# Block 1's edge pass of a graph network on one Trainium2 core: two products in bf16 with three-part factors instead of fp32

## The reference, cut to what matters

```python
def _L1_gnn_ref(x, edge_index, W, b):
    row, col = (edge_index[0], edge_index[1])
    msg = jax.nn.relu(jnp.concatenate([x[row], x[col]], axis=-1) @ W.T + b)
    agg = jax.ops.segment_sum(msg, row, num_segments=x.shape[0])
    out = jax.nn.relu(jnp.concatenate([x, agg], axis=-1) @ W.T + b)
```

## Time and profile before

| | us |
|---|---|
| median of 3 runs | 16247.92 (16245.1 to 17099.07) |
| the profiled execution, its time | 16245.7 |
| its span | 16244.0 |
| DVE busy / ACT busy / POOL busy / PE busy | 6528.5 / 5590.2 / 10961.6 / 8570.5 |
| phase e1, from TensorE's first transpose to ScalarE's last copy | 5065.01 to 5971.29 |

### The profile page before, as it was taken

The page is one execution under the profiler, slowest core; times in us unless marked ns, Lnnn a source line. Parts: engine busy times, 40 slices in busy tenths (PEclk is TensorE's granted clock), DMA queues, the critical chain, the costliest instruction groups (busy, mean ns, idle before and its releaser), DMA issues. The chain is left out here.

```text
span 16244.0 us, 250527 instructions
## 1 busy us (share of the span) xinstructions
PE 8570.5 (53%) x72124; PEld 7859.4 (48%) x72124; DVE 6528.5 (40%) x23629; ACT 5590.2 (34%) x12958; POOL 10961.6 (67%) x11452
## 2 busy tenths in 40 slices
PE   6555541655656974444432433442444444788886
PEld 4555541555556973333332333331444443677775
DVE  5555553877773544333335333335222224111112
ACT  2555541777772321222221222220121222333332
POOL 4777767677773017777767777766777773777773
PEclk9777665878788985666665666665555555899996
DMA  4444431322223542444432444442232231444441
GB/s 148 147 149 148 149 120 50 103 92 92 92 92 116 184 139 83 145 146 148 145 121 71 146 148 145 145 143 51 83 86 84 84 86 46 141 147 146 148 145 53
DMA packets 883633, 1910.02 MB, mean 118 GB/s; under 512 B 379346, under 2 KB 458529, under 8 KB 842333
## 3 DMA queue, kind: packets, MB, share of 16 engines
q0 software_dynamic: 361472, 581.36, 14.2%
q1 hardware_dynamic: 414093, 743.26, 14.2%
q10 hardware_dynamic: 107776, 582.40, 9.0%
HBM read 1071.64 MB, written 863.86 MB: 119 GB/s over the span
## 5 line engine op out<-in xcount | busy, mean ns | idle before, releaser
L112 POOL DMA_INDIRECT eg_got<-gat_table,eg_rows x4992 | 4715.9, 945 | 1541.5 <-issue 1500.6
L112 POOL DMA_INDIRECT e_got<-table,e_rows x3328 | 3150.4, 947 | 1028.5 <-issue 1001.9
L1299 PE MATMUL eg_ps_sum<-eg_got,eg_equal 128*128 128x136 f32 (+1 forms) x9984 | 2073.1, 382 | 277.8 <-DVE eg_got L1387 257.5
L1306 ACT ACTIVATE eg_outs<-eg_ps_sum 128x544 f32<-128x544 f32 (+1 forms) x1248 | 676.2, 542 | 4266.8 <-PE eg_ps_sum L1299 4255.6
L1299 PEld LDWEIGHTS eg_ps_sum<-eg_got,eg_equal 128*128 128x128 f32 x9984 | 1968.1, 291 | 341.4 <-ACT eg_outs L1306 184.3
L117 POOL DMA_INDIRECT sorted_rows<-sort_rows,sort_dest x1664 | 1616.3, 971 | 533.8 <-issue 499.2
L1331 PE MATMUL eg_small<-ident,eg_score 128*128 128x128 f32 (+1 forms) x312 | 138.6, 444 | 3162.7 <-DVE eg_score L1370 3162.7
L1331 PEld LDWEIGHTS eg_small<-ident,eg_score 128*128 128x128 f32 (+1 forms) x312 | 47.1, 151 | 3190.2 <-DVE eg_score L1370 3190.2
L1368 DVE TENSOR_TENSOR eg_diff<-eg_small,eg_got 128x128 f32<-128x128 f32 (+1 forms) x312 | 79.0, 253 | 2725.8 <-DMA eg_got<-gat_table,eg_rows 2725.8
L1565 DVE TENSOR_SCALAR e_got<-e_ps_second 128x512 f32<-128x512 f32 x416 | 287.7, 692 | 1825.3 <-PE e_ps_second L1548 1797.9
L567 PE MATMUL e_ps_sum<-e_got,e_equal 128*128 128x64 f32 x3328 | 627.5, 351 | 675.3 <-DMA e_got<-table,e_rows 675.3
(11 more groups left out here) (520 smaller groups left out, 21698.4 us busy)
## 6 DMA issues: line engine op xcount, KB each, us to landing
gat_out<-eg_outs ACTq DMA_DIRECT2D x208, 1152.0 KB
eg_equal_b<-equal_d SPq DMA_DIRECT2D x312, 512.0 KB
out<-e_outs ACTq DMA_DIRECT2D x208, 512.0 KB
out<-e_outs ACTq DMA_DIRECT2D x104, 1024.0 KB
values_q<-e_zeros_b SPq DMA_DIRECT2D x104, 768.0 KB
sort_value<-values_q SPq DMA_DIRECT2D x104, 768.0 KB
eg_got<-gat_table,eg_rows POOLq DMA_INDIRECT x4992
gat_out<-eg_outs ACTq DMA_DIRECT2D x104, 528.0 KB
```

What stands on the lines that cost most here:

```text
L112: return e.indirect_dma_start(out, None, table, bass.IndirectOffsetOnAxis(ap=index, axis=0), **kw)
L1299: last_i = e.matmul(ps_sum[q % 2][:, i, 0:FG], equal[q % 4][:, i, :], got[k][:, t, :], start=True, stop=True)
L1306: e.activation(outs[k % 2][:, tiles, 0:FG], ps_sum[q % 2][:, :, 0:FG], ACT.Copy).then_inc(copied.sem, 1)
```

## The change

Both products of e1 use bf16 zeros and ones and three bf16 parts of the other factor, three products each summed in PSUM. `values1` and the table by node hold own parts as three bf16 parts, cut in `split` by VectorE. In e1 the message is cut on the way: ScalarE writes part 1 (relu, bf16), VectorE the fp32 rest (`less`), ScalarE part 2, GpSimd part 3. The reach of the steps is eight, `equal` has 16 buffers, `cut` eight, `rest` four. `rows` are reloaded after `rests` and not after the sums. `keys.load` goes from GpSimd's start of e1 to the end of SyncE's loop. The fp32 own parts stay in `feat[:, :, D:2D]`, so that b1c loads no table.

```diff
-        self.values1 = self.dram("values1", (EP, D))
+        self.values1 = self.dram("values1", (EP, 3 * D), BF16)
-        zeros = ph.sb("zeros", [P, GT * D])
+        zeros = ph.sb("zeros", [P, GT * HEADS])
-                    clear(self.values1, zeros)
+                    clear(self.values1, zeros_b)
...
-        value = [ph.sb(f"value{k}", [P, GT, D]) for k in G4]
-        equal = [ph.sb(f"equal{k}", [P, QT, P]) for k in range(RING)]
+        value = [ph.sb(f"value{k}", [P, GT, 3 * D], BF16) for k in G4]
+        equal = [ph.sb(f"equal{k}", [P, QT, P], BF16) for k in range(U)]
+        cut = [ph.sb(f"cut{k}", [P, 3, QT, D], BF16) for k in range(CUTS)]
+        rest = [ph.sb(f"rest{k}", [P, QT, D]) for k in G4]
...
 def sync(e):  # in the loop, and after it
-                    e.wait_ge(summed.sem, summed.at(it, (k + 1) * QUADS - U))
+                    e.wait_ge(less.sem, less.at(it, (k + 1) * QUADS - U))
+            keys.load(e)
...
+            def spread_rows(it, q):
+                e.wait_ge(equaled.sem, equaled.at(it, q + 1))
+                e.wait_ge(added.sem, added.at(it, q - 1))
+                for i in range(QT):
+                    for a in range(3):
+                        last_i = e.matmul(ps_fill[q % 2][:, i, 0:D], equal[q % U][:, i, :], value[k][:, tiles.start + i, a * D:(a + 1) * D],
+                                          start=a == 0, stop=a == 2)
+            def sums(it, q):
+                e.wait_ge(cut_3.sem, cut_3.at(it, q + 1))
+                e.wait_ge(copied.sem, copied.at(it, q - 1))
+                for i in range(QT):
+                    for a in range(3):
+                        last_i = e.matmul(ps_sum[q % 2][:, i, 0:D], equal[q % U][:, i, :], cut[q % CUTS][:, a, i, :],
+                                          start=a == 0, stop=a == 2)
+            stepped(e, (8, spread_keys), (6, spread_rows), (0, sums))
...
+            def rests(it, q):
+                e.wait_ge(cut_1.sem, cut_1.at(it, q + 1))
+                e.wait_ge(cut_3.sem, cut_3.at(it, q + 1 - n4))
+                e.scalar_tensor_tensor(rest[q % 4][:, :, :], rows[k][:, tiles, 1:], 0.0, cut[q % CUTS][:, 0], ALU.max, ALU.subtract).then_inc(less.sem, 1)
+            stepped(e, (3, rests), (5, add), (7, compare))
...
+            def first_part(it, q):
+                e.wait_ge(added.sem, added.at(it, q + 1))
+                e.wait_ge(summed.sem, summed.at(it, q + 1 - CUTS))
+                e.activation(cut[q % CUTS][:, 0], rows[k][:, tiles, 1:], ACT.Relu).then_inc(cut_1.sem, 1)
+            def second_part(it, q):
+                e.wait_ge(less.sem, less.at(it, q + 1))
+                e.activation(cut[q % CUTS][:, 1], rest[q % 4][:, :, :], ACT.Copy).then_inc(cut_2.sem, 1)
+            stepped(e, (2, second_part), (4, first_part), (0, copy_sums))
...
+            def third_part(it, q):
+                e.wait_ge(cut_2.sem, cut_2.at(it, q + 1))
+                e.tensor_tensor(cut[q % CUTS][:, 2], rest[q % 4][:, :, :], cut[q % CUTS][:, 1], ALU.subtract).then_inc(cut_3.sem, 1)
-            keys.load(e)
+            stepped(e, (1, third_part))
...
 def split(e, i, ts, n, ps):  # b0c; own = self.feat[:, :, D:2 * D]; waits left out
+            e.tensor_copy(m3[:, :, 0], own_n).then_inc(lin.out, 1)
+            e.tensor_tensor(ro[:, 0], own_n, m3[:, :, 0], ALU.subtract).then_inc(lin.out, 1)
+            e.tensor_copy(m3[:, :, 1], ro[:, 0]).then_inc(lin.out, 1)
+            e.tensor_tensor(ro[:, 1], ro[:, 0], m3[:, :, 1], ALU.subtract).then_inc(lin.out, 1)
+            e.tensor_copy(m3[:, :, 2], ro[:, 1]).then_inc(lin.out, 1)
...
-            e.dma_start(own, nodes(table_p)).then_inc(own_in, 16)
-            e.wait_ge(own_in, 16)
```

More of the change, by code:

```diff
@@ L1049, in carried_pass @@
         ph = Phase(self.nc, "e1")
-        tiles = TileValues(self, ph, 1, self.table_p, values)
+        tiles_in = TileValues(self, ph, 1, self.table_p3, values)
         keys = TileKeys(self, ph, 1, by_group(self.sorted_rows), F32)
@@ L1067, in carried_pass @@
         spread = Tally(ph, "spread", U)
-        equaled = Tally(ph, "equaled", U, ahead=len(G4))
+        equaled = Tally(ph, "equaled", U, ahead=n4)
         fills = Tally(ph, "fills", U, ahead=U)
         added = Tally(ph, "added", U, ahead=2)
-        message = Tally(ph, "message", U)
+        cut_1 = Tally(ph, "cut_1", U)
+        less = Tally(ph, "less", U, ahead=U)
+        cut_2 = Tally(ph, "cut_2", U)
+        cut_3 = Tally(ph, "cut_3", U, ahead=n4)
         summed = Tally(ph, "summed", U, ahead=U)
@@ L1077, in place, with stepped, step, tensor @@
             k, i = divmod(q, QUADS)
[L1078 to L1083, removed]
+            return k % n4, slice(i * QT, (i + 1) * QT), k // n4
+        def stepped(e, *parts):
+            def step(it, s, end=None):
+                for reach, part in parts:
+                    if s + reach >= 0 and (end is None or s + reach < end):
+                        part(it, s + reach)
+            for s in range(-max(reach for reach, part in parts), 0):
+                step(0, s)
             with e.Fori(0, TURNS - 1) as it:
[L1085 to L1088, removed]
+                for s in range(U):
+                    step(it, s)
+            for s in range(U):
+                step(TURNS - 1, s, U)
         def sync(e):
             e.dma_start(group_f[:, :], rows_v[:, 0, :, 0]).then_inc(group_in, 16)
-            tiles.sync(e)
+            tiles_in.sync(e)
             with e.Fori(0, TURNS) as it:
                 for k in G4:
-                    g = bass.ds(it * len(G4) + k, 1)
+                    g = bass.ds(it * n4 + k, 1)
                     e.wait_ge(fills.sem, fills.at(it, (k + 1) * QUADS - U))
                     e.dma_start(value[k][:, :, :], values_v[g, :, :, :].rearrange("g p t c -> (g p) t c")).then_inc(loaded[k].sem, 16)
-                    e.wait_ge(summed.sem, summed.at(it, (k + 1) * QUADS - U))
+                    e.wait_ge(less.sem, less.at(it, (k + 1) * QUADS - U))
                     e.dma_start(rows[k][:, :, :], rows_v[g, :, :, :].rearrange("g p t c -> (g p) t c")).then_inc(loaded[k].sem, 16)
-        def pe_step(e, it, n, real):
-            q = n + 5
-            if real(q):
+            keys.load(e)
+        def tensor(e):
+            def spread_keys(it, q):
                 k, tiles, turn = place(q)
@@ L1174, in vector, with copy_sums @@
             e.sem_inc(added.sem, added.ahead)
-            staged(e, dve_step)
+            e.sem_inc(less.sem, less.ahead)
+            stepped(e, (3, rests), (5, add), (7, compare))
             keys.links(e)
         def scalar(e):
+            def first_part(it, q):
+                k, tiles, _ = place(q)
+                e.wait_ge(added.sem, added.at(it, q + 1))
[4 more added lines that the diff above has]
+                e.activation(cut[q % CUTS][:, 1], rest[q % 4][:, :, :], ACT.Copy).then_inc(cut_2.sem, 1)
+            def copy_sums(it, q):
+                k, tiles, _ = place(q)
+                e.wait_ge(summed.sem, summed.at(it, q + 1))
+                e.wait_ge(stored[k % 2].sem, stored[k % 2].at(it, k // 2))
+                e.activation(outs[k % 2][:, tiles, :], ps_sum[q % 2][:, :, 0:D], ACT.Copy).then_inc(copied.sem, 1)
+                if q % QUADS == QUADS - 1:
+                    e.wait_ge(copied.sem, copied.at(it, q + 1))
+                    g = bass.ds(it * n4 + k, 1)
+                    e.dma_start(out_v[g, :, :, :].rearrange("g p t c -> (g p) t c"), outs[k % 2][:, :, :]).then_inc(stored[k % 2].sem, 16)
+                    for a in B2:
+                        e.dma_start(ends_v[g, a, :, :], outs[k % 2][a * (P - 1):a * (P - 1) + 1, :, :]).then_inc(stored[k % 2].sem, 16)
             for k in B2:
@@ L1999, in close0_open1 @@
         bias = ph.sb("bias", [P, D])
-        own = ph.sb("own", [P, NT, D])
-        other = ph.sb("other", [P, NT, 3, D], BF16)
-        rest = ph.sb("rest", [P, 2, QT, D])
+        own = self.feat[:, :, D:2 * D]
+        other, mine = (ph.sb(k, [P, NT, 3, D], BF16) for k in ("other", "mine"))
+        rest, rest_own = (ph.sb(k, [P, 2, QT, D]) for k in ("rest", "rest_own"))
         collect = Collect(self, ph, agg, 0, out)
@@ L2006, in close0_open1 @@
         w_in, tables_out, added = ph.sem("w_in"), ph.sem("tables_out"), ph.sem("added")
-        lin = ChunkLinear(self, ph, "lin", self.feat[:, :, 0:D], w[:, :, :].rearrange("i a o -> i (a o)"), 2 * D, 6, norm.ready)
-        others = other[:, :, :, :].rearrange("p t a c -> p t (a c)")
-        spread = SpreadStarts(self, ph, 1, own, self.values1, "own")
+        lin = ChunkLinear(self, ph, "lin", self.feat[:, :, 0:D], w[:, :, :].rearrange("i a o -> i (a o)"), 2 * D, 11, norm.ready)
+        others, mines = (a[:, :, :, :].rearrange("p t a c -> p t (a c)") for a in (other, mine))
+        spread = SpreadStarts(self, ph, 1, mines, self.values1, "own")
         spread_q = SpreadStarts(self, ph, 0, others, self.values_q, "other")
@@ L2081, in block1 @@
         ins = self.ins
```

(2 more changed lines are left out.)

86 lines of the change are left out of this document (29 added, 57 removed).

## The result

| | before | after |
|---|---|---|
| median of the runs, us | 16249.47 (4 runs) | 16093.53 (4 runs, 16089.35 to 16123.38) |
| the profiled execution, its span | 16244.0 | 16121.7 |
| e1, first transpose to last copy | 906.3 | 748.7 |
| e1, start to start of the first and last keys, per quad | 898.5, 2.160 | 737.3, 1.772 |

The ratio is 0.9908, 95% interval 0.9896 to 0.9921: the median is 156 us lower, which stays within the 2% of the prediction. One of the four runs of the kernel before took 17099.07 us and is not in the ratio. The forecast gain in e1 was 212 us, the measured one 158.

The account below looks back on a forecast made before the run. TensorE alone was taken to bound e1 before the change. The profiled 16245.7 us, less 212 in e1, plus 9 in b0c, gave 16043 us; the range was 15945 to 16165.

Parts of the forecast that it names:

- the port: In e1, `rests` waits for GpSimd's subtraction after a group's end: 1.49 us in place of 1.14, 1.65 per quad.
- The chain: In e1, ScalarE's issues delay part 1, so VectorE waits 1.14 us per group: 6.26 us, 1.57 per quad.
- TensorE's products: In e1, each bf16 product takes 0.35 us; with the transposes TensorE needs 1.14 us per quad.
- VectorE's step: In e1, `rests`, addition and comparison take 0.34 + 0.34 + 0.60 = 1.28 us per quad.
- ScalarE's step: In e1, two parts and the copy take 0.92 us per quad; with the issues 5.30 per group, 1.33 per quad.
- GpSimd's subtraction: In e1, one subtraction of 256 elements takes 0.68 us, the middle between 0.45 and 0.91.
- Fill and tail: In e1, filling has ten hops, some 6 us, and a larger first load; 8 us added.
- The DMA floor of 1.47: In e1, 1.84 MB per group at 312 GB/s take 5.9 us, 1.47 per quad, close under 1.65.
- rival 1: Nothing couples in e1: a quad takes 1.33 to 1.50 us, the kernel 15909 to 15980 us; chance 0.13.
- b0c: Extra casts and subtractions in `split` add 45 us of VectorE work, which costs the phase +9, bounds 0 and 45.
- Rival 2: Each e1 step loses the port: a quad takes 1.85 to 2.10 us, the kernel 16126 to 16230; chance 0.17.
- Rival 3: TensorE's clock falls to 1.2 GHz in e1: a quad takes 2.28 us, the kernel 16305; chance 0.05.

Follow-up runs that it names:

- longer order: The changed kernel with the addition two steps further ahead of `rests` and ScalarE's part 1 one step: e1's keys 572.2 and 575.7 us, kernel 15935.31 us.
- the run with nearly nothing else left: The kernel with the longer order, loading half the values after the first turn and without GpSimd's third part: e1's keys 534.1 us, 1.284 per quad.
- the run with five issues: The changed kernel with ScalarE issuing the two small transfers of each group a second time: e1's keys 876.8 us, 2.108 per quad.

## Why the prediction was right, point by point

The mechanism came as forecast, and one term of the sum, the port, did not: it made the gain in e1 158 us instead of 212. The range was wide enough to hold that.

- **The chain, as forecast.** ScalarE's issues block it (1.52 and 1.56 seen, 1.53 taken), and VectorE then waits 1.09 and 1.14 in the group shown and 1.24 in the mean of 104 (1.14 computed). Without the port I gave 1.57 per quad; the run without the third part has 1.579. More issues, fewer issues and a longer order all move it as the chain says.
- **TensorE's products** start 0.36 and 0.35 us before the next work (5400.05, 5400.41, 5400.76), as taken. Its busy share is 75% and not 69%, because the profile counts 0.52 and 0.51 us for them.
- **VectorE's step** was 1.28; the timeline has 1.26, and the run with nearly nothing else left 1.284.
- **ScalarE's step** was taken at 0.92 and has 0.88 to 0.90 behind its issues. So its 1.33 per quad was no floor: the last run of e1 has 1.284 with all of ScalarE's work in it.
- **GpSimd's subtraction**: 0.68 taken, 0.67 measured where it is alone. The estimate from the page's figures and the earlier trace rows was 0.72 (the Trainium skill, GPSIMD Engine Reference, Performance versus the Vector engine), and the trace lies nearer to the middle of my bounds.
- **The port was mis-sized, and it is the error.** I let most steps lose nothing and the late one 0.35 us, so 0.35 per group. The timeline has 0.28 + 0.50 = 0.78 in one group, and the run without the subtraction gives 82 us or 0.79. The difference of 0.44 is 46 of the 55 us by which e1 was longer than the forecast; 6 are the chain (1.579 against 1.565) and 3 the filling. What I missed is the catching up: behind its issues ScalarE works back to back for three steps, and the subtraction, 0.88 us after the one before while a step takes 1.54, drifts through the step until it starts 0.04 us ahead of a `rests`. I had followed the late chain for one step only. That whichever starts first holds the other up (the Trainium skill, SBUF — State Buffer, Who interferes with whom) is borne out in both directions, `rests` going from 0.41 to 0.91 and the subtraction from 0.67 to 0.89.
- **Fill and tail** took 11 us, 8 were taken.
- **The DMA floor of 1.47 was wrong** but decided nothing. I scaled 58.6% at 183 GB/s to 312 GB/s; 343 were moved at 0.96, a quad of 1.342. Shares of different traffic do not scale by their GB/s: q1 moved 3.7 KB a packet in the earlier trace rows and moves 4.6 now (110.57 MB in 24137 packets). Had TensorE and VectorE been quicker, the error would have counted, since rival 1's upper end stood on it.
- **b0c: +9 predicted, +2 measured** (507.2 to 509.4 us from e0's last keys to sort1's first product). The gathers, which I had expected at 1.2 us, stay at 1114 ns. The scatters of the other parts take 28 ns more; that the added VectorE work causes it is likely but not shown. e0 got 2 to 3 us, within its bounds of -1 and +5.
- **Rivals.** Rival 1 (1.33 to 1.50) is what the longer order gives, 1.375: my argument against it, "nobody can use that slack ahead of time" was a fact of the written order only. Rival 2's 1.85 was not reached: two steps in four lose to the port, not all. Rival 3: the clock did dip with TensorE less busy, 0.97 at 75% and 0.90 in the run with five issues at 68%, but TensorE was not the bound at either, and it never stayed at 0.50. My argument against it, that at half the clock e1 would be busy without a pause and rise again, was wrong for the old e1, as the last section shows.
- **The sum.** 157.6 us gained in e1, 5 lost ahead of it; the medians differ by 156. The 3 us between are not accounted for.

## What to carry to other kernels

When an engine stops being the bound, look for stalls on its neighbours that its lateness used to cover: three DMA issues per group on ScalarE cost nothing before, and have VectorE wait 129 us after. Whether a stall costs depends on how many steps the order leaves between producer and reader, so that changing five numbers in three lines was worth nearly as much as moving the work to another queue. The two together won less than either: the loads then had less time, and came late. When two engines can hold one another up, follow the late engine until it has caught up, not for one step.

## What the runs showed of the hardware

- The old e1, with TensorE busy for 440.00 of 440 us, ran at a granted clock of 0.50 (1.2 GHz) from 6699.5 to 8416.6, 1717 us instead of 898.5: being busy without a pause did not raise it. The kernel before took 17099.07, 17076.39 and 17077.42 us in three of its 11 runs on the first kind of chip. Those left no trace, but the mean clock of the last two is on record, 0.664 and 0.666 against 0.70, and e1 at 0.50 instead of 1.00 would make it 0.664 (an estimate from these rows). None of 14 runs with the bf16 e1 on such chips was longer than 16124 us; whether its pauses are the reason no run shows.
- A pair of small DMA issues took 0.68 us on ScalarE, and a pair right behind it 1.42.
- `rests`, 0.41 us alone, ends 0.28 us after a subtraction of GpSimd's that had started before it.
